# Reordering the last transposes, the projection in and the token centring in the scan layers of a four-layer vision kernel

## The reference, cut to what matters

```python
h = _layernorm(x, n1_g, n1_b)
p = h @ w_in + b_in                                   # 96 -> 192 channels
local = conv_general_dilated(p, k_conv, ..., feature_group_count=inner)   # 3x3, depthwise
lr = _ema_scan(local, axis=2)
rl = _ema_scan(local, axis=2, reverse=True)
tb = _ema_scan(local, axis=1)
bt = _ema_scan(local, axis=1, reverse=True)
mixed = 0.25 * (lr + rl + tb + bt) + local
mixed = _layernorm(mixed, on_g, on_b)
x = x + (mixed @ w_out + b_out)
h2 = _layernorm(x, n2_g, n2_b)
m = gelu(h2 @ w1 + b1) @ w2 + b2                      # 96 -> 384 -> 96
return x + m
```

## Time and the profile before

| | |
|---|---|
| time before, median of 3 runs | 3452.87 us (3451.18 to 3456.98) |
| the profiled execution | 3447.74 us |
| its span, first to last instruction | 3446.0 us |
| span of the scan layers, about | 3006 to 3446 us |
| PE busy / DVE busy / ACT busy / POOL busy, whole span | 88% / 73% / 52% / 30% |

### The profile page before, as it was taken

One profiled execution on the slowest core, in us unless ns is written; L12 is line 12 of the kernel. 1 busy time (PEld: TensorE's weight loads), 2 busy tenths in 40 slices (PEclk: granted clock), 3 DMA queues, 4 the chain that ended last, 5 costly groups with the idle time before them and its releaser, 6 DMA issues. The chain is left out here.

```text
span 3446.0 us, 136025 instructions
## 1 busy us (share of the span) xinstructions
PE 3044.3 (88%) x50244; PEld 2301.4 (67%) x50244; DVE 2529.0 (73%) x12095; ACT 1807.9 (52%) x5562; POOL 1035.4 (30%) x2516
## 2 busy tenths in 40 slices
PE   5449999999957989999999999999999999568887
PEld 1136666666622439888889888889888898345554
DVE  4539999999963847777777777777777777578873
ACT  1239999999923145444445444444444454234443
POOL 0027778777710012222222222222222222100000
PEclk9769999999968985555555555555555555579998
DMA  1243333333330000000000000000000000000000
GB/s 35 82 142 98 105 111 111 114 111 99 102 90 19 0 1 4 5 5 5 5 5 4 5 5 5 5 5 5 5 5 5 5 4 5 12 0 1 1 6 14
DMA packets 54533, 115.50 MB, mean 34 GB/s; under 512 B 12313, under 2 KB 19801, under 8 KB 53692
## 3 DMA queue, kind: packets, MB, share of 16 engines
q1 hardware_dynamic: 37216, 53.87, 5.5%
q0 software_dynamic: 13824, 50.34, 4.0%
q10 hardware_dynamic: 2844, 2.70, 0.4%
HBM read 84.06 MB, written 22.81 MB: 31 GB/s over the span
## 5 line engine op out<-in xcount | busy, mean ns | idle before, releaser
L534 PE MATMUL g_zr<-g_hp,g_wp 97*128 97x4 f16 x24576 | 1081.5, 171 | 70.1 <-issue 65.9
L534 PEld LDWEIGHTS g_zr<-g_hp,g_wp 97*128 97x128 f16 x24576 | 955.1, 108 | 178.9 <-issue 69.5
L642 POOL COPY s_y<-g_hs 96x8 f32 x2048 | 398.1, 194 | 1324.0 <-DVE g_hs L585 1324.0
L625 ACT ACTIVATE g_e<-g_tn 96x8 f32<-96x8 f32 x2048 | 436.4, 213 | 556.4 <-DVE g_tn L570 556.4
L583 DVE TENSOR_TENSOR_SCAN g_hp<-g_gates,g_e 96x16 f16<-96x16 f32 x2048 | 384.7, 188 | 316.9 <-ACT g_e L625 209.8
L510 PE MATMUL g_zr<-s_inner,g_wi 96*128 (+2 forms) x6240 | 582.9, 234 | 3.2 <-DVE g_hs L560 3.1
L622 ACT ACTIVATE g_gates<-g_zr 96x16 f32<-96x16 f32 x2048 | 401.4, 196 | 297.4 <-PE g_zr L534 297.2
L898 DVE CUSTOM_DVE_ANT_0 a_negated<-a_scores,a_mask 128x1024 f32<-128x1024 f32 x384 | 468.2, 1220 | 85.3 <-DMA a_mask<-in_L_mask 44.6
L541 PE MATMUL g_n<-g_hp,g_wp 97*128 97x8 f16 x8192 | 520.2, 174 | 0.0
L924 ACT ACTIVATE a_probs<-a_negated,a_negmax 128x1024 f32<-128x1024 f32 x384 | 442.2, 1152 | 25.8 <-DVE a_negmax L898 16.1
L570 DVE TENSOR_TENSOR_SCAN g_tn<-g_gates,g_n 96x24 f32<-96x24 f32 x2048 | 388.5, 190 | 73.5 <-ACT g_gates L622 73.3
(11 more groups left out here) (318 smaller groups left out, 3271.8 us busy)
## 6 DMA issues: line engine op xcount, KB each, us to landing
a_mask<-in_L_mask POOLq DMA_DIRECT2D x96, 512.0 KB, 5.5
a_k<-k_rows SPq DMA_DIRECT2D x96, 144.0 KB
q_rows<-r_q_parts SPq DMA_DIRECT2D x12, 576.0 KB, 7.3
k_rows<-r_k_parts SPq DMA_DIRECT2D x12, 576.0 KB, 7.5
a_q<-q_rows SPq DMA_DIRECT2D x96, 72.0 KB
o_parts<-a_o_sb SPq DMA_DIRECT2D x384, 18.0 KB
o_part<-o_parts SPq DMA_DIRECT2D x32, 192.0 KB
out_x<-x SPq DMA_DIRECT2D x4, 384.0 KB, 3.0
```

The lines of the kernel that those rows point to most:

```text
L534: mm = pe.matmul(zr_bank[u, k][:, 1 - g, d, :, at], wp[0:97, part, (2 * u + d) * NG + g, :], hp[u][0:97, d * NB:(d + 1) * NB, e], start=False,
L625: act.activation(e1[u][:, :, 0], tn[u][:, :, 2], ACT.Tanh, scale=to_tanh).then_inc(n_and_zh[u], 1)
L642: po.tensor_copy(yv[:, 2 * u:2 * u + 2, :, bass.ds(token, 1)], h.unsqueeze(3)).then_inc(y_ok[u], 1)
```

## The change

Three lists are reordered; no instruction is added or taken away. On PE, the last two transpose pairs (6 and 7) of e come ahead of `project_in(f, 0)` instead of between the two halves of the projection. On ACT, the copies of these pairs come ahead of `take_in(f, 0)` instead of between `take_in(f, 0)` and `take_in(f, 1)`. On DVE, `centre_tokens(e, 1)` comes straight behind `centre_tokens(e, 0)`, and taps 2 and 3 come behind both. PE's and ACT's part takes effect where f and e are both there (slots 2 to 7), DVE's where v and e are (slots 2 to 8).

```diff
@@ PE
                         spread_half(ring[h], h, f_parts, f_spread)
-                    project_in(f, 0)
                 if e is not None:
                     turn_pairs(e, range(6, 8))
                 if f is not None:
+                    project_in(f, 0)
                     project_in(f, 1)
@@ ACT
                     take_turns(e, range(4, 6))
+                if e is not None:
+                    take_turns(e, range(6, 8))
                 if f is not None:
                     if f >= 2:
                         act.wait_ge(tapped, 2 * TAPS * (f - 1))
                     take_in(f, 0)
-                if e is not None:
-                    take_turns(e, range(6, 8))
-                if f is not None:
                     take_in(f, 1)
@@ DVE
                 if e is not None:
                     centre_tokens(e, 0)
+                    centre_tokens(e, 1)
                 if v is not None:
                     taps(v, 2, 4)
-                if e is not None:
-                    centre_tokens(e, 1)
```

## The result

The changed kernel took 3463.31 us (median of 10 runs, 3460.7 to 3466.1) beside 3451.73 us for the kernel before (10 runs, 3449.72 to 3461.49): a ratio of 1.003, 95% interval 1.002 to 1.0039. It is 11.6 us slower, where the forecast was 3452.2 and the range ended at 3459.

What follows compares the result with a forecast made beforehand. No engine was full in the scan layers; list order and the chain of waits bound the kernel, 45.12 us a slot. Gain 3.9 less clock loss 3.2 leaves 0.7: 3452.87 - 0.7 = 3452.2 us, range 3434 to 3459.

Steps and rivals of the forecast that it cites:

- the early mix: On PE, the mix starts at T + 5.8 instead of T + 9.55 at the high clock, 3.7 us earlier.
- POOL held back: POOL's add, released among ten back-to-back taps, stays out until the last ends and finishes at T + 24.76, as before.
- the new wait: PE idles up to 3.4 us ahead of the variance of e, waiting for POOL's add.
- T: Start of the f_xn product on DVE in a slot; the prediction counts the slot's times from it.
- The 3.9 us of gain: Sum over slots before clock losses: 0.6 in slots 3, 4, 5, 7; 1.7 in slot 6; 1.6 in slot 8.
- The mix of a slow slot: On PE with the projection at the low clock, the mix gains between 0.2 and 1.9 us; 1.0 was taken.
- I expect two of six slots to pay: 3.2: Slow clock behind PE's wait ahead of the variance costs 3.2 us in all, set against the 3.9 gain.
- about 1.6 us: Price of one low-clock stretch at PE's variance and second product, taken from slot 6's slow mix, 1.57 us.
- rival 2: Clock drops behind PE's new wait in all six slots: 5.7 to 16 us slower, 3459 to 3469 us; chance 0.08.
- Rival 1: POOL's add gets in between two of DVE's taps: 13 to 26.5 us faster, 3440 to 3426 us; chance 0.26.
- Rival 3: The order does nothing; another wait keeps PE's mix at T + 9.5: 3452.9 us; chance 0.04.

Runs made afterwards that it cites:

- the kernel with PE kept busy: Changed kernel plus five unused products of 384 columns on PE ahead of its wait for POOL's sum, in slots with v: 3452.02 us, ratio 0.9999 to before.
- the one with the variance over both tiles: Changed kernel without POOL's add; PE's variance of e takes 16 products over both tiles' squares instead of 8 over their sum: 3436.02 us, ratio 0.9955 to before.

## Why the prediction was wrong

Its path held: the early mix, POOL held back, the new wait. Its count and its price of the slow stretches of PE did not.

**What held.** The mix came to T + 5.81 (T + 5.8 predicted). POOL's add started at T + 17.63 (T + 17.9), stayed out until the taps were done, and ended 2.20 us behind the last of them at T + 24.76, exactly where the prediction had it. PE waited 3.74 us ahead of the variance (up to 3.4 was said), and the variance moved from T + 24.99 to T + 24.81 (T + 24.83). Slot 2 kept its length (0 predicted). Slot 8's variance came 1.64 us earlier (1.6). The 3.9 us of gain were never measured by themselves: 1.7 of them, slot 6's, follow only if its slow stretch cost what those of slots 4, 5 and 7 did, and the kernel with PE kept busy shows 1.2 us in these slots. The mix of a slow slot was off too, without effect: the prediction gave it 0.2 to 1.9 us and took 1.0, and in slot 3 it came at T + 7.13, 2.4 us earlier.

**What failed** is the step "I expect two of six slots to pay: 3.2", and the price in it of "about 1.6 us" a stretch. All six slots from 3 to 8 paid. Where the wait was 3.74 us the variance took 1.89 us more and the second product 0.89 more, 2.78 together, in slots 4 to 7. In slots 3 and 8, with waits of 2.27 and 2.37 us, the price was 1.64 + 0.16 = 1.8 and 0.14 + 1.64 = 1.8. The sum is 4 x 2.78 + 2 x 1.8 = 14.7 us, less the gain of 3.9 = 10.8, which is the difference of the two stretches (slots 2 to 8 alone add 10.7 in the table). This is rival 2, at a price between its two ends (1.6 and 3.3 each), to which a chance of 0.08 was given. It was to decide from a cost of 6.9 + 3.9 = 10.8 us; the cost was 14.7.

Two pieces of reasoning stood behind the wrong step. The first took the price from one row, the slow mix tile of slot 6, 1.57 us, behind which the next product was at its usual length again. Behind the new wait the low clock lasted into the second product, and both rows are on the chain. The rows of slots 2 and 9 of the kernel before, above, showed the dearer case; 3.3 us stood in rival 2 alone. What sets how long such a stretch lasts is not shown, and it is not the length of the wait by itself: behind the same 3.74 us the kernel with PE's and ACT's part alone lost 1.74 us on the mix tile and 0.41 on the product behind it, in slot 5, where the changed kernel lost 1.89 and 0.89. The second reasoned that slots with a slow projection would have little wait left, and that a fall would come there or at the variance, by turns. In the changed kernel it came at the variance each time. The projection ran at the high clock in four of the five slots from 3 to 8 that have one, so the mix was early there and the wait behind it was full. Slots 4 to 6 repeat one another to within 0.1 us (47.68, 47.74, 47.75). The mixture of fast and slow projections that the kernel before shows did not last once a longer idle stretch stood elsewhere in the loop.

**The clock at the projection.** The prediction expected that transposes in the gap ahead of the projection would not keep the clock. In slots 4 to 7 the clock was kept, in slot 3 it fell. That is no verdict for the transposes: PE's wait there was 1.32 us and not the 2.24 of before, and the clock had been low behind the wait for POOL in the slot before. With the same order on PE the projection was fast and slow by turns in the kernel with PE's and ACT's part alone, and partly slow in slots 3 to 7 of the one with the variance over both tiles. The Trainium skill's rule, in TensorE: Matmul & The Clock Gate, section PE-mode transpose, that transposes don't count as busy for the clock in the way that matmuls do, is neither borne out nor refuted by these rows.

**Rival 1, POOL between two taps.** It did not happen in the changed kernel: through adds of 5.66 to 8.05 us POOL passed up two to four ends of a tap instruction before the last. It happened once a reciprocal or a tensor_tensor stood among the taps, and then its time came as well: 3421 us, somewhat beyond its best case of 3426. The rule in the Trainium skill's SBUF — State Buffer, section Who interferes with whom, that DVE with two SBUF inputs and a reading GpSimd instruction exclude each other, agrees with every run (an add of 2.35 us grows to 7.14, or a tap of 1.27 to 3.37). Its issue order does not tell who goes next at the end of a tap: in the row of ten taps the waiting POOL did not, behind a 0.19 us reciprocal it did.

**Rival 3**, no effect of the order, was out with the mix at T + 5.81.

**What stays open** is why a row of taps keeps POOL out. Number of SBUF inputs, length of the gap, a wait and a semaphore are ruled out as the cause, each by a run; what is left of those tried is the kind of the instruction, or its 96 partitions, since the three that let POOL in were over 128 and the scalar_tensor_tensor over 96 like the taps. The tap instruction that gives way is the first to the third behind such an instruction; m_xn on DVE (L1910, a tensor_tensor over 96 partitions, one input in PSUM) stands right ahead of the ten taps, and six tap instructions later they don't. How long the effect of an instruction lasts, no run tells. What sets the clock's fall at the projection, slot by slot, is open as well.

## What to carry to other kernels

An earlier product is worth what the slowest link behind it lets through: follow it to the next engine, and ask whether that engine shares a port with one that is now busy. When a wait on PE moves, price the clock behind its new place by the dearest slow stretch that the trace shows, in every turn of the loop, and look first for a slot that already waits at that place. The kernel to use is the change with the small reciprocal between taps 6 and 7, or with DVE's wait for POOL's sum there: 3421 us, 0.991 of before, where the order alone gives 1.003.

## What the hardware showed that was not expected

- POOL's tensor_tensor of 96x1024 with both inputs in SBUF takes 2.34 us alone, and 5.28 to 9.36 us when it is released inside a row of scalar_tensor_tensor instructions on DVE with two SBUF inputs each: it gets no turn at the ends of two to five of them before the last, although it is waiting.
- One reciprocal of 0.19 or 0.94 us or one tensor_tensor of 0.95, over 128 partitions, in that row turns this round, and a scalar_tensor_tensor of 1.21 us over 96 does not: in the slots with m POOL takes 2.35 to 3.24 us, and one of the three tap instructions behind takes 2.50 to 3.37 us instead of 1.27.
- Behind a wait of 3.74 us PE ran at 0.50 of its clock for the variance and the start of the next product, 2.78 us lost, in four slots alike; behind 2.3 us it lost 1.8. The length of the wait alone does not set the price: 2.6 us were lost behind a wait of 2.93 us, and 2.15 behind another of 3.74.
